# Four-field tiles multiplied twice in the second cross layer of a CIN recommender kernel, and first-layer operands by loads instead of by TensorE

## The reference

```python
B, F, D = (512, 39, 16)
H1, H2 = (128, 128)
...
e = emb_table[feat_index]
flat = e.reshape(e.shape[0], -1)
linear_part = flat @ linear_w + linear_b
x0 = e
h1 = jax.nn.relu(jnp.einsum('bhd,bmd,ohm->bod', x0, x0, conv_w1) + conv_b1[None, :, None])
nxt, hi1 = jnp.split(h1, 2, axis=1)
h2 = jax.nn.relu(jnp.einsum('bhd,bmd,ohm->bod', nxt, x0, conv_w2) + conv_b2[None, :, None])
res = jnp.concatenate([hi1, h2], axis=1).sum(axis=2)
y = jax.nn.relu(_bn(flat @ deep_w1 + deep_b1, bn_g1, bn_b1))
y = jax.nn.relu(_bn(y @ deep_w2 + deep_b2, bn_g2, bn_b2))
cat = jnp.concatenate([linear_part, res, y], axis=1)
return cat @ out_w + out_b
```

## Time and profile before

| | us |
|---|---|
| median of 3 runs (461.06 to 463.33) | 461.39 |
| the profiled execution | 462.93 |
| its span, first to last instruction | 461.1 |
| TensorE busy | 408.9 |
| VectorE busy | 367.7 |
| GpSimd busy | 296.2 |
| ScalarE busy | 196.5 |

### The profile page before, as it was taken

The page is one execution under the profiler, slowest core; times in us unless marked ns, Lnnn a source line. Parts: engine busy times, 40 slices in busy tenths (PEclk is TensorE's granted clock), DMA queues, the critical chain, the costliest instruction groups (busy, mean ns, idle before and its releaser), DMA issues.

```text
span 461.1 us, 4691 instructions
## 1 busy us (share of the span) xinstructions
PE 408.9 (89%) x1228; PEld 227.9 (49%) x1228; DVE 367.7 (80%) x406; ACT 196.5 (43%) x252; POOL 296.2 (64%) x221
## 2 busy tenths in 40 slices
PE   0037976998799999989999999999999999979996
PEld 0013432454355465555555556556557555654572
DVE  5353866777778888788989899997893998899894
ACT  0322216107412471465247523742563346475543
POOL 4777777677478058797689777851586248428472
PEclk9999999999899999999999999999999999999999
DMA  6354789679999789999899989999957997899770
GB/s 158 45 103 73 199 198 212 122 169 204 241 222 213 131 217 253 242 227 233 185 225 223 229 185 203 229 235 256 242 135 189 227 228 180 213 238 240 183 183 2
DMA packets 47516, 88.65 MB, mean 192 GB/s; under 512 B 18940, under 2 KB 24379, under 8 KB 47489
## 3 DMA queue, kind: packets, MB, share of 16 engines
q1 hardware_dynamic: 33545, 80.97, 72.5%
q0 software_dynamic: 5120, 1.32, 6.3%
q10 hardware_dynamic: 8823, 6.05, 6.1%
HBM read 87.03 MB, written 1.28 MB: 192 GB/s over the span
## 4 chain that ended last, share of the span: by engine, by line
PE 60%; DMA 11%; POOL 9%; DVE 6%; issue 6%; ACT 3%; SPq 3%; POOLq 1%; ACTq 1%; DVEq 0%
PE p_h L898 36%; PE p_n L898 14%; POOL G L595 7%; PE p_x L878 5%; DMA ring<-xs_scratch 4%; DMA xs_scratch<-xT 4%; PE p_x L966 4%; DVE ring L732 2%; DMA G<-in_emb,idx_all 2%; POOL zl L609 2%; SPq L517 2%; DMA w1s<-in_w1a 1%; ACT zh L1095 1%; SPq L543 1%; DVE zl L700 1%
## 5 line engine op out<-in xcount | busy, mean ns | idle before, releaser
L595 POOL DMA_INDIRECT G<-in_emb,idx_all x160 | 167.4, 1047 | 49.4 <-issue 43.5
L609 POOL TENSOR_TENSOR zl<-ring,zh 128x1024 fp32r<-128x1024 f32 (+1 forms) x52 | 121.1, 2340 | 108.0 <-ACT zh L1095 96.8
L732 DVE TENSOR_TENSOR ring<-p_n,ring 128x1024 f32<-128x1024 f32 (+1 forms) x167 | 177.8, 1094 | 12.6 <-ACT p_n L1124 6.2
L898 PE MATMUL p_h<-ring,w2s 128*128 128x512 f32 x286 | 136.3, 604 | 5.3 <-DVE ring L732 4.5
L1095 ACT ACTIVATE zh<-ring 128x1024 fp32r<-128x1024 f32 (+1 forms) x79 | 80.7, 1029 | 136.9 <-DVE ring L732 134.5
L898 PE MATMUL p_n<-placed,w1s 125*128 125x512 f32 (+2 forms) x192 | 93.3, 607 | 0.0
L732 DVE TENSOR_TENSOR placed<-xa,p_x 125x1024 f32<-125x1024 f32 (+5 forms) x51 | 57.2, 1121 | 40.3 <-PE p_x L878 40.0
L898 PEld LDWEIGHTS p_h<-ring,w2s 128*128 128x128 f32 x286 | 55.2, 195 | 59.2 <-issue 47.4
L898 PE MATMUL p_h<-zh,w2l 128*128 128x512 f32 x169 | 65.7, 466 | 2.3 <-ACT h2s L1132 1.2
L878 PE MATMUL p_x<-stack,put 103*125 103x512 f32 (+3 forms) x117 | 55.3, 547 | 12.8 <-DVE stack L705 11.1
L898 PE MATMUL p_h<-zh,w2h 128*128 128x512 f32 x169 | 54.0, 397 | 0.0
(11 more groups left out here) (107 smaller groups left out, 279.0 us busy)
## 6 DMA issues: line engine op xcount, KB each, us to landing
ring<-xs_scratch SPq DMA_DIRECT2D x258, 256.0 KB, 6.7
ring<-xs_scratch SPq DMA_DIRECT2D x76, 128.0 KB, 3.8
xa<-xs_scratch ACTq DMA_DIRECT2D x21, 156.0 KB
G<-in_emb,idx_all POOLq DMA_INDIRECT x160
xs_scratch<-xT ACTq DMA_DIRECT2D x16, 64.0 KB
dw_sb<-in_dw SPq DMA_DIRECT2D x4, 200.0 KB
xa<-in_dw ACTq DMA_DIRECT2D x2, 156.2 KB
xa<-xs_scratch SPq DMA_DIRECT2D x4, 78.0 KB
```

The source lines that it names most:

```text
L595: nc.gpsimd.indirect_dma_start(G[:, b % 2, DIM * f:DIM * (f + 1)], None, emb[:, :], bass.IndirectOffsetOnAxis(index_of(b, f), 0)).then_inc ...
L609: nc.gpsimd.tensor_tensor(low_of(s), z_of(s), high_of(s).bitcast(F32), ALU.subtract).then_inc(s_low_pool, 1)
L732: nc.vector.tensor_tensor(z_of(s), by, x, ALU.mult).then_inc(s_z, 1)
L898: return nc.tensor.matmul(acc[:, BANK * c:BANK * (c + 1)], w, x[:, BANK * c:BANK * (c + 1)], start=start, stop=stop)
```

## The change

**L2.** A tile now has four fields by 32 rows. The 64 outputs of n stand twice in `p_n`, so partitions 32c to 32c + 31 meet field 4i + c with one half of n (kind `a`), and, against `p_sw`, where the halves are swapped, the same loaded tile meets the other half (kind `b`). Nine such tiles are loaded once each (`load_quad`, 4 DMAs of 32 rows) and used twice: kind `a` writes its product to a new ring `zr` of 5 buffers, kind `b`, later, multiplies in place. Fields 36, 37 make a tile as before (kind `l`), field 38 the tail (kind `t`). Each part still has 20 L2 tiles, with 11 loads instead of up to 20.

**L1.** The 6 tiles are products of 2 own operands (`own`, fields m and m + 9, 127 rows) and 3 partner operands (`rooms`, kind `P`), all loaded (3 DMAs of 39 rows and one of 10, 4 in all). ScalarE copies the own operand into PSUM (`own_in_psum`). There is no `place`, `stack`, `put1`, `high_x`, `low_x`, `copy_fields`. Eighteen of the 39 scratch rows are written a second time (`AGAIN`), so that cyclic runs need no wrap.

**Buffers.** `rooms` has 12 buffers with fixed users: nine for the `X` loads, one shared by `P` 0 and `T`, one by `P` 1 and `L`, one for `P` 2. `p_n` is a single buffer; `p_sw` has the place of the second. `n` leaves `p_n` by way of SBUF (`n_sb`) and takes 4 ScalarE passes, and 4 more of 32 rows (`swapped_n`).

**Order.** L1 tiles of part j + 1 are at (j, 11), (j, 12), (j, 13), (j, 16), (j, 17), (j, 18) in every stretch; kinds a, t, l at places 0 to 10; kind b at 14, 15 and 19 to 25. The scratch writes of parts 2 to 8 go from ScalarE's queue to SyncE's. Split tiles, in units of 1024 tokens, by stretch from 3 on: 9, 9, 10, 15, 16, 16 before; 8, 7, 8, 13, 12, 7 now.

```diff
+OWNS, PARTNERS, SHIFT, EXTRA = 2, 3, 9, 10
+X_TILES = OWNS * PARTNERS
+AGAIN = 2 * SHIFT
+_MAIN = [(g, m) for g in range(3) for m in range(FIELDS)]
+OWN = [[m + SHIFT * a for _, m in _MAIN] for a in range(OWNS)]
+PARTNER = [[m + SHIFT + 3 * t + 1 + g for g, m in _MAIN] for t in range(PARTNERS)]
+for _r in reversed(range(EXTRA)):
+    OWN[0].append(18 - 2 * _r)
+    OWN[1].append(FIELDS + 17 - 2 * _r)
+    PARTNER[0].append(38 - 2 * _r)
+    PARTNER[1].append(37 - 2 * _r)
+    PARTNER[2].append(36 - 2 * _r)
...
-X_AT = {0: [5, 7, 8, 14, 17, 20], 1: [6, 7, 9, 14, 15, 20], 2: [3, 8, 9, 15, 16, 18], 3: [0, 2, 4, 8, 12, 13],
...
+FIRST_TILES = [('a', 0), ('a', 1), ('a', 2), ('t', TAIL), ('l', LAST)] + [('a', i) for i in range(3, QUADS)]
+X_AT = [11, 12, 13, 16, 17, 18]
...
+DVE_LOW = {-1: [], 0: [3, 7, 15], 1: [3], 2: [3, 23], 3: [3, 9, 10, 19, 23], 4: [3, 19, 21, 24], 5: [3, 7, 9, 19, 20, 24], 6: [3, 5, 10, 15, 21, 23], 7: [3, 24], 8: [2, 3, 5, 7, 18]}
...
-POOL_LOW = {-1: [], 0: [19], 1: [10], 2: [5], 3: [1, 3, 7, 11, 16, 21], 4: [1, 3, 11, 16, 21],
...
+T_PE_AT = {0: 20, 1: 20, 2: 1, 3: 1, 4: 1, 5: 1, 6: 1}
+T_ACT_AT = {0: 22, 1: 22, 2: 3, 3: 3, 4: 3, 5: 3, 6: 3}
...
-HI_BEHIND, DUP_BEHIND, N_BEHIND, HI_SUM_BEHIND, H2_PLACE, H2_SUM_PLACE = 3, 6, 7, 5, 1, 6
-LOW_BEHIND, COPY_AHEAD, PLACE_AHEAD = 1, 3, 6
-RING, PLACED_RING, HIGH_RING, LOW_RING = 8, 4, 6, 7
...
+OWN_AT = (7, 14)
+SQ_ACT_AT, SQ_DVE_AT = 11, 15
+HI_BEHIND, DUP_BEHIND, N_BEHIND, HI_SUM_BEHIND, H2_PLACE, H2_SUM_PLACE = 3, 3, 3, 5, 0, 6
+SWAP_AT, LAST_SWAP_AT = (2, 4, 6, 8), (9, 9, 9, 9)
+LOW_BEHIND = 1
+Z_RING, HIGH_RING, LOW_RING = 5, 5, 6
...
+def room_of(what, t):
+
+    return {'X': t, 'P': QUADS + t, 'T': QUADS, 'L': QUADS + 1}[what]
+
+
+def last_reader(what, b, t):
+
+    return INDEX[{'X': ('b', b, t), 'P': ('x', b, PARTNERS + t), 'T': ('t', b, TAIL), 'L': ('l', b, LAST)}[what]]
+
...
+def loads_of(j):
+
+    own = [('O', j + 2, 0), ('O', j + 2, 1), ('P', j + 2, 2)] if j + 2 < PARTS else []
+    rest = [('P', j + 2, 0), ('P', j + 2, 1)] if j + 2 < PARTS else []
+    early = own if j >= EARLY_OWN else []
+    write = [('W', j + 2, 0)] if 0 <= j < PARTS - 2 else []
+    out = write if j >= EARLY_OWN else []
+    if j + 1 < PARTS:
+        out = out + [('X', j + 1, 0), ('X', j + 1, 1), ('X', j + 1, 2), ('T', j + 1, 0), ('L', j + 1, 0), ('X', j + 1, 3)]
+        out += early + [('X', j + 1, i) for i in range(4, QUADS)]
+    return out + (write + own if j < EARLY_OWN else []) + rest
+
...
-        p_n = [ps("p_n0", [128, TOK]), ps("p_n1", [128, TOK])]
+        p_n = ps("p_n", [128, TOK])
+        p_sw = ps("p_sw", [128, TOK])
...
+        def load_rows(eng, dst, b, values, landed):
+
+            for p, n, first, step in field_runs(values):
+                eng.dma_start(dst[p:p + n, 0:TOK_OF[b]], xs_rows(b, first, n, step)).then_inc(landed, 16)
...
+        def load_quad(eng, b, i):
+
+            if b:
+                for c in range(4):
+                    eng.dma_start(rooms[QUAD * c:QUAD * (c + 1), i, 0:TOK_OF[b]], xs_rows(b, 4 * i + c, QUAD, 0)).then_inc(s_room[i], 16)
...
+        def load_last(eng, b):
+            room = room_of('L', 0)
+            for half in range(2):
+                eng.dma_start(rooms[NEXT * half:NEXT * (half + 1), room, 0:TOK_OF[b]],
+                              xs_rows(b, 4 * QUADS + half, NEXT, 0)).then_inc(s_room[room], 16)
+
+        def load_tail(eng, b):
+            room = room_of('T', 0)
+            eng.dma_start(rooms[:, room, 0:TOK_OF[b]], xs_rows(b, FIELDS - 1, 128, 0)).then_inc(s_room[room], 16)
...
-            for m, s in enumerate(LOADED):
+            for what, b, t in LOADS:
+                if what == 'W':
+                    own_wait(sp, s_x, X_COPIED[b])
+                    scratch_write(sp, b, XS_WRITES[b])
+                    continue
+                if b > written:
+
+                    own_wait(sp, s_xs, XS_LANDED[b])
+                    written = b
+                if what == 'O':
+                    if b == 0:
+                        continue
+                    own_wait(sp, s_own, OWNS * (b - 1) + t + 1)
+                    if t == 0:
+                        own_wait(sp, s_sq, b)
+                    load_own(sp, b, t)
+                    continue
+                before = BEFORE[what, b, t]
+                if before:
+                    wait_used(sp, last_reader(*before))
+                if what == 'X':
+                    load_quad(sp, b, t)
+                elif what == 'P':
+                    load_partner(sp, b, t)
+                elif what == 'T':
+                    load_tail(sp, b)
+                else:
+                    load_last(sp, b)
+                if (what, b, t) == ('P', HALVES + 1, 1):
+                    for early in range(HALVES):
+                        load_flat(sp, early)
                     load_deep()
...
+                if s in RINGED and RINGED.index(s) >= Z_RING:
+                    wait_used(dve, RINGED[RINGED.index(s) - Z_RING])
+                if kind == 'x':
+                    a, t = divmod(t, PARTNERS)
+                    room = room_of('P', t)
+                    dve.wait_ge(s_room[room], LANDED['P', b, t][1])
+                    dve.wait_ge(s_own, OWNS * b + a + 1)
+                    if a:
+                        dve.wait_ge(s_z, INDEX['x', b, t] + 1)
+                    x = rooms[0:r, room, cols]
+                    by = (p_h2 if b == 0 and a else p_x)[0:r, cols]
+                elif kind == 'b':
+                    dve.wait_ge(s_swap, 4 * (b + 1))
+                    dve.wait_ge(s_z, INDEX['a', b, t] + 1)
+                    x, by = z_of(s), p_sw[:, cols]
                 else:
-                    a = PLACED.index(s)
...
+                    load = {'a': ('X', b, t), 'l': ('L', b, 0), 't': ('T', b, 0)}[kind]
+                    room = room_of(load[0], load[2])
+                    dve.wait_ge(s_room[LANDED[load][0]], LANDED[load][1])
                     dve.wait_ge(s_n, b + 1)
-                    by = p_n[b % 2][:, 0:TOK_OF[b]]
+                    x, by = rooms[:, room, cols], p_n[:, cols]
                 nc.vector.tensor_tensor(z_of(s), by, x, ALU.mult).then_inc(s_z, 1)
 
...
-            def place(s):
...
+                    if first and b:
+                        pe.wait_ge(s_z, LAST_A[b - 1] + 1)
+                        pe.wait_ge(s_swap, 4 * b)
...
-            def load_fields(b):
+            def own_in_psum(b, a):
+
+                sc.wait_ge(s_own_in[a], OWN_LANDED[a] * (b + 1))
...
+                if b:
+                    own_wait(sc, s_z, INDEX['x', b, PARTNERS - 1] + 1 if a else LAST_X[b - 1] + 1)
+                cols = slice(0, TOK_OF[b])
+                nc.scalar.activation((p_h2 if b == 0 and a else p_x)[0:OWN_ROWS, cols], own[:, a, cols], ACT.Copy).then_inc(s_own, 1)
...
-            def high_x(b):
...
-            def copy_fields(s):
...
             def second_n(b):
 
+                sc.wait_ge(s_sq_low, b + 1)
+                cols = slice(0, TOK_OF[b])
+                nc.scalar.activation(n_sb[:, cols], p_n[0:NEXT, cols], ACT.Relu, bias=b1_dup[0:NEXT, :]).then_inc(s_n_sb, 1)
                 sc.wait_ge(s_hi, b + 1)
+                sc.wait_ge(s_n_sb, b + 1)
+                nc.scalar.activation(p_n[NEXT:128, cols], n_sb[:, cols], ACT.Copy).then_inc(s_dup, 1)
+
+            def first_n(b):
+
                 cols = slice(0, TOK_OF[b])
-                nc.scalar.activation(p_n[b % 2][NEXT:128, cols], p_n[b % 2][0:NEXT, cols], ACT.Relu,
-                                     bias=b1_dup[NEXT:128, :]).then_inc(s_dup, 1)
-
-            def first_n(b):
-
-                sc.wait_ge(s_dup, b + 1)
+                nc.scalar.activation(p_n[0:NEXT, cols], n_sb[:, cols], ACT.Copy).then_inc(s_n, 1)
+
+            def swapped_n(b, c):
+
+                if c == 0:
+                    sc.wait_ge(s_n, b + 1)
+                    if b:
+                        sc.wait_ge(s_z, L2_OF[b - 1][-1] + 1)
+                    if b == PARTS - 1:
+                        sc.wait_ge(s_pre, 2 * HID_T)
                 cols = slice(0, TOK_OF[b])
-                nc.scalar.activation(p_n[b % 2][0:NEXT, cols], p_n[b % 2][0:NEXT, cols], ACT.Relu,
-                                     bias=b1_dup[0:NEXT, :]).then_inc(s_n, 1)
+                nc.scalar.activation(p_sw[QUAD * c:QUAD * (c + 1), cols], n_sb[QUAD * (1 - c % 2):QUAD * (2 - c % 2), cols], ACT.Copy).then_inc(s_swap, 1)
 
...
```

521 lines of the change are left out of this document (211 added, 310 removed).

## The result

| | us |
|---|---|
| kernel before, median of 4 runs (460.34 to 463.33) | 461.23 |
| kernel after, median of 4 runs (506.62 to 519.44) | 515.07 |
| ratio, 95% interval | 1.105 [1.091, 1.118] |
| the profiled execution of after, and its span | 517.13, 515.3 |
| predicted | 454.4 (438 to 466) |

A forecast was written before the change was run, and what follows sets the result against it. It took TensorE to bound the kernel, with loads as a new limit in the stretches 2 to 5: TensorE's end at 439.4, plus 14.7 lost to loads, plus 0.3 from span to median, gives 454.4 us (438 to 466).

The forecast's parts named there:

- What a tile costs on TensorE: All stretches: a plain tile 1.71 us, split 1.41, tail 0.94, dense 4.30 or 3.44; stretches 3 to 5 42.6, 42.9, 42.6.
- the `p_sw` rival: Stretch 8: b tiles wait for `p_sw`, held by the dense layer until (8, 8); 457 to 462 us, chance 0.10.
- TensorE may wait some 8 us at (1, 11); the gather covers that too: First quarter: part 2's L1 operands load late, but gathers hide the wait; TensorE at (2, 2) at 117.5 us.
- the cover: First quarter: the gather hides TensorE's wait at (1, 11) with about 9 us to spare.
- the 2.6 us of idle: First quarter: GpSimd's earlier wait for ScalarE, expected to go with its low parts later in the tables.
- SyncE's own 4 x 0.30 a load is hidden below 2.13: Chain of loads: SyncE's issue time for a load's four DMAs hides behind the load's 2.13 us.
- No term for stretch 2: Stretch 2: TensorE's own 39.8 us from (2, 2) on; no term for the moved write of part 3.
- A load takes 2.13 us: Stretches 3 to 5: 14 loads take 29.8 us, from windows of full DMA queues at 251 and 242 GB/s.
- The rival of slow loads: Loads at (3, 12), (4, 12), (5, 12): 2.46 us each or uneven rows, 462.5 us; both 471; chance 0.27.
- No loss there: From (5, 19) to (6, 12) and later: 32.2 us of loads hide behind 37.8 us of TensorE's own work.
- X 2 of the next part waits: X 2 waits for b 2 at (j, 19), starting a burst of 14 loads until P 1; chain 34.1 us.
- Hidden work: ScalarE's 2 to 4 us more a stretch, the single `p_n` and VectorE's 43.2 to 44.6 us stay hidden.

The follow-up runs named there:

- e2: Kernel after with the nine X loads of parts 3 to 8 bringing 16 columns instead of 1024, issues kept; 482.8 us.
- e3: Kernel after with the five own and partner loads of parts 3 to 8 bringing 16 columns instead of 1024, issues kept; 483.2 us.
- e9: e1 with the own loads and P 2 of part 2 also moved from SyncE's to ScalarE's queue; 523.3 and 533.1 us.
- e15: Kernel after with scratch writes of parts 2 to 8 and own loads and P 2 of part 2 on ScalarE's queue, as in e9; 524.4 us.
- e17: Kernel after with no GpSimd low part in stretch 1, tiles (1, 7) and (1, 15) contracted plain; 508.9 us, 1.105 of before.
- e1: Kernel after with the scratch writes of parts 2 to 8 back on ScalarE's queue; 496.4 us, 1.068 of before.
- e14: Kernel after with every own and partner load as 4 DMAs of 32 rows; 522.0 us where before took 497.3.
- e13: Kernel after, unchanged, run again in the job of e14; 533.2 us where before took 497.3.
- e18: e15 plus own and partner loads of 32 rows, late dense-layer loads and no GpSimd low part in stretch 1; 484.9 us, 1.049 of before.
- e10: Kernel after with all own and partner loads as 4 DMAs of 32 rows, the edit of e14 in another job; 522.1 us.

## Why the prediction was wrong, by its steps

**What a tile costs on TensorE: right.** 43.0 and 42.7 in e2 and e3, for 42.9 and 42.6. Stretches 6 and 7 without load waits take 52.0 and 53.4, of it 1.4 and 2.4 idle, so 50.6 and 51.0 for 49.6 and 49.5. Stretch 8 with its tail took 54.0 for 54.9; the `p_sw` rival did not come.

**"TensorE may wait some 8 us at (1, 11); the gather covers that too": this step failed first, and TensorE was at (2, 2) 21 us late.** It saw the right place and priced the wait at half (14.4), and the cover of "about 9 us" was a number without a sum. Without the 2.7 us for the gathers TensorE would have been at (2, 2) at 135.9, 27 us behind the 108.5 that the cover implies. The longer wait is 6.4 of that, the later start at (0, 0) 3.9, the lower clock in stretch 1 some 6 (below); the rest is many short waits in stretches 0 and 1 that had no term either. The low parts of GpSimd, from which the prediction expected the 2.6 us of idle to go, waited 1.8 and 16.5 us. SyncE's issues were costed as "SyncE's own 4 x 0.30 a load is hidden below 2.13". That is a load of 1024 tokens and 0.30 from a lone DMA. In stretch 1 a load has 512 tokens, so half the data (1.07 us at the same rate), and 24 issues took 12.18 us, 0.51 each, 2.03 us a load: there the issues are the limit. The own and `P` loads of part 2 stand behind them and behind the write that the change put on the same queue. The sum counted SyncE's order for stretches 3 to 5 alone and gave the moved writes no term. e9 and e15 show the queue's order as the cause of this wait, e17 that the gathers only follow it.

**No term for stretch 2: 14 us.** The write of part 3 was not followed to ScalarE's next use of `xT`, so that who waits for a moved DMA had its answer on another engine (13.6 us). e1 gives back 3 to 6 us here and about 17 in all.

**"A load takes 2.13 us": mis-sized, 2.9 to 3.1 measured in stretch 4.** The mechanism was right, a burst of loads after (j, 19) that ends later than TensorE needs it, but its rate came from windows in which before's queue was always full, mostly of even loads of 64 rows. For even loads it stands (2.02 in e14). The rival of slow loads had 2.46 or a quarter more for five of 14, both together 471. It named the form of the loads as a cause, which e14 shows for stretches 6 and 7, and gave it too small a size. Also "No loss there" for stretches 6 and 7 (32.2 us of loads against 37.8) fails by this term alone: 14 loads of 3.1 are 43, and of 2.9 still 41. The place was (j, 6), since at 3.1 us `X` 4 behind `O` and `P` is late already.

**"X 2 of the next part waits": the burst had 16 loads.** `X` 0 comes free only with GpSimd's low part of (j, 14), and the queue is in order.

**The clock had no price.** Windows of after around the waits at (3, 6) and (4, 6), columns as above:

```profile
200.00:207.00 7.00, 2.52 (x6) 0.76 (x4) 0.00 (x0) 0.00 (x0) 0.00 (x0) 1.00 1.04 235
207.00:214.00 7.00, 3.90 (x8) 2.32 (x9) 6.26 (x5) 4.13 (x4) 3.80 (x3) 0.51 0.92 241
255.00:262.00 7.00, 2.43 (x6) 0.76 (x4) 2.35 (x2) 1.07 (x2) 0.00 (x0) 0.98 0.96 220
262.00:268.00 6.00, 5.50 (x9) 3.00 (x10) 4.27 (x4) 3.06 (x3) 5.09 (x4) 0.50 0.87 196
```

TensorE works a third of the seven microseconds, and in the next seven the granted clock is 0.5, its lower level of 1.2 GHz. Only what TensorE does at that level costs time: 3.9 us busy at 0.51 is some 1.9 us of work less, so the idle gap of 7.1 us cost about 9; after the one of 4.6 us at (4, 6) it is 5.5 us busy at 0.50, some 2.7. After the 14.4 us at (1, 11) the first three tiles took 8.2 us for 5.1 by the prices. So each such gap was followed by 2 to 3 us of loss. The means of stretches 1 and 2 (0.77 of 52.9 us, 0.86 of 60.6) hide that TensorE stood through much of the low clock, at 0.50 from 99 to 109 us for one. Counted over short windows, by its busy time alone, some 6 us are lost in each, 12 together (an estimate), against at most 1.6 in each of before's first three stretches (clock 0.95, 0.96 and 0.97) and nothing from stretch 3 on (1.00).

**Hidden work: right.** ScalarE's swaps and copies, the single `p_n`, VectorE's 43 to 45 us: nothing of this shows in e2's stretches 4 and 5.

## What to carry to other kernels

A change that cuts bytes but turns a steady stream of loads into bursts is priced by the order of the queue: write down, place by place, every DMA that stands ahead of the one that is waited for, the moved ones too, with its issue time at the size it has there. Take the rate of a load from rows of the same form, and give a known rule on the form of a DMA a price in the sum until a row speaks against it. Put 2 to 3 us on top of every gap of some five microseconds or more, for the clock behind it, as measured here.

## What was not expected of the hardware

SyncE's issue time of the same DMA is not fixed. The first 12 `X` DMAs of part 1 that stand in one row took 17.25 us in e13, 1.4 each, and 6.08 in e18, 0.51 each:

```profile
75.94 17.25 SPq L554 DMA_DIRECT2D rooms<-xs_scratch  x12
```

```profile
67.81 6.08 SPq L554 DMA_DIRECT2D rooms<-xs_scratch  x12
```

In the profiled execution of after the same row took 6.07 us. It was so in both traces of these jobs that were read for it (16.39 us in e10), together with waits of up to 14 us ahead of TensorE's weight loads that are put down to nothing (14.3 in e13, 0.5 in after, 1.7 in e17, though 12.1 in e18); in stretches 6 and 7 of e13 the longest of them was 1.1 us. The jobs in which the kernel before took 497 to 509 us ran on other chips. What differs there was not found.
